# Where four query products of the next block stand: two in the attention steps and two behind output projection, or all four behind it

## The reference, cut to what matters

```
h = layernorm(x)                                # x: 4 x 2048 rows of 512
q = h @ Wq.T                                    # 1024 columns: 2 x 16 heads of 32
k, v = ctx @ Wk.T, ctx @ Wv.T                   # 154 context rows, 8 key/value heads
w = softmax(q1 k1) - lam * softmax(q2 k2)
a = (w v) * rsqrt(mean((w v)^2) + eps) * g * (1 - LAMBDA_INIT)
x = x + a @ Wo.T
h = layernorm(layernorm(x)) * g1 + b1ln         # second norm, then the norm inside the FFN
f = layernorm(gelu(h @ ternary(W1).T + b1))     # 2048 hidden columns
x = x + f @ ternary(W2).T + b2
```

## Time and profile before

| | |
|---|---|
| three runs | 2541.35, 2542.62, 2545.44 us (median 2542.62) |
| the profiled execution's span | 2537.8 us |
| PE, share of the span | 92% |
| DVE | 66% |
| ACT | 53% |
| POOL | 40% |
| HBM traffic | 36 GB/s over the span |

### The profile page before, as it was taken

One profiled execution on the slowest core, in us unless ns is written; L12 is line 12 of the kernel. 1 busy time (PEld: TensorE's weight loads), 2 busy tenths in 40 slices (PEclk: granted clock), 3 DMA queues, 4 the chain that ended last, 5 costly groups with the idle time before them and its releaser, 6 DMA issues.

```text
span 2537.8 us, 39240 instructions
## 1 busy us (share of the span) xinstructions
PE 2324.9 (92%) x13663; PEld 1092.8 (43%) x13663; DVE 1668.2 (66%) x2714; ACT 1340.0 (53%) x1943; POOL 1008.9 (40%) x823
## 2 busy tenths in 40 slices
PE   8489998999999898999989899998989999898988
PEld 5243544435353443535344353534435353444433
DVE  3866757485775748567574856757486675756563
ACT  3325465554656455465645546564554656465455
POOL 0221534435253443525344352534435253433416
PEclk9679999999999999999999999999999999999999
DMA  7222122120312212031221203122120312212000
GB/s 259 72 63 62 46 62 63 51 58 17 96 27 67 57 56 63 8 95 27 68 56 56 68 3 95 27 68 56 56 69 2 95 27 68 56 39 69 25 11 17
DMA packets 150890, 144.79 MB, mean 57 GB/s; under 512 B 66216, under 2 KB 117988, under 8 KB 150220
## 3 DMA queue, kind: packets, MB, share of 16 engines
q1 hardware_dynamic: 150732, 142.36, 19.6%
HBM read 70.56 MB, written 20.36 MB: 36 GB/s over the span
## 4 chain that ended last, share of the span: by engine, by line
PE 38%; issue 31%; DVE 14%; POOL 11%; ACT 4%; DMA 1%; POOLq 0%; SPq 0%; ACTq 0%; DVEq 0%
PE ps L1253 14%; PE ps L1263 13%; PE ps L1158 4%; DVE attn_raw L891 4%; POOL rstd L457 2%; POOL arena L481 2%; POOL q L462 2%; POOL arena L494 1%; POOL arena L490 1%; POOL rows L462 1%; DVE arena L853 1%; PE ps L1121 1%; ACT arena L642 1%; DVE attn_raw L886 1%; DVE p L873 1%
## 5 line engine op out<-in xcount | busy, mean ns | idle before, releaser
L494 POOL TENSOR_TENSOR arena<-arena 128x512 f32<-128x512 f32 x448 | 560.9, 1273 | 340.4 <-ACT arena L649 339.6
L1253 PE MATMUL ps<-rows,w1T 128*128 128x512 f16 x2048 | 484.5, 381 | 12.2 <-DVE rows L945 12.2
L853 DVE TENSOR_REDUCE arena<-ps 128x3 f32<-128x462 f32 (+1 forms) x704 | 405.4, 618 | 124.7 <-PE ps L1158 123.0
L1263 PE MATMUL ps<-w2T,arena 128*128 128x512 f16 x2048 | 478.8, 379 | 0.0
L642 ACT ACTIVATE arena<-ps,vec_cols,wstep 128x512 f32<-128x512 f32 x256 | 199.7, 780 | 447.4 <-PE ps L1253 404.2
L950 DVE SCALAR_TENSOR_TENSOR arena<-arena,vec_cols 128x512 f16<-128x512 f32 x256 | 196.9, 769 | 234.2 <-ACT arena L647 232.8
L1253 PEld LDWEIGHTS ps<-rows,w1T 128*128 128x128 f16 x2048 | 192.2, 98 | 216.1 <-DVE rows L945 21.6
L595 ACT ACTIVATE arena<-ps 128x512 f32<-128x512 f32 x128 | 76.2, 595 | 395.3 <-PE ps L1123 392.4
L1263 PEld LDWEIGHTS ps<-w2T,arena 128*128 128x128 f16 x2048 | 195.1, 98 | 207.1
L1158 PE MATMUL ps<-k_max,stack_raw 96*128 96x154 f16 x2048 | 208.4, 234 | 26.9 <-DVE arena L853 24.8
L462 POOL TENSOR_TENSOR q<-arena,q 128x512 f16<-128x512 f32 x64 | 74.2, 1160 | 396.5 <-ACT q L597 396.5
(11 more groups left out here) (163 smaller groups left out, 3387.1 us busy)
## 6 DMA issues: line engine op xcount, KB each, us to landing
arena<-in_x SPq DMA_DIRECT2D x32, 1024.0 KB, 6.1
stack_raw<-rows SPq DMA_DIRECT2D x384, 64.0 KB, 2.0
stack_raw<-q SPq DMA_DIRECT2D x384, 64.0 KB, 2.0
out<-arena SPq DMA_DIRECT2D x64, 256.0 KB, 2.1
arena<-in_L_ffn_w SPq DMA_DIRECT2D x8, 1024.0 KB, 10.6
k_max<-k_store SPq DMA_DIRECT2D x16, 490.0 KB
k_att<-k_store SPq DMA_DIRECT2D x16, 490.0 KB
v_att<-v_store SPq DMA_DIRECT2D x16, 384.0 KB, 5.8
```

The source lines that it names most:

```text
L494: ins = pool.tensor_tensor(acc[:, e, :], acc[:, e, :], src[:, j % 2, :], ALU.add)
L853: dve.tensor_reduce(negmax[:, tt, u0:u1], ps[:, B_O + tb % 2, 0:(u1 - u0) * S].rearrange("p (u s) -> p u s", s=S), AX.X, ALU.max, negate=T ...
L1253: ins = pe.matmul(ps[:, B_H + j % 2, :], w1T[:, k, j * P:(j + 1) * P], rows16[:, e, k, :], start=(k == 0 and e == 0), stop=(k == KD - 1 an ...
L1263: ins = pe.matmul(ps[:, tt, :], gg16[:, j % 3, e, tt * P:(tt + 1) * P], w2T[:, j, :], start=(j == 0 and e == 0), stop=(j == JH - 1 and e = ...
```

## The change

Two of the eight query products leave the attention steps, and a third moves one step later there. `q3` stands behind `v4` instead of `v3`; `q4` and `q5` stand behind output projection, ahead of `q6` and `q7`. The four late products alternate between two banks: `q5` moves to `B_L`, where `q7` is. The waits follow the banks: `q6` waits for the copy of `q4`, `q7` for that of `q5`. In the prologue `q5` waits for the row maxima of the first share, since it now shares their bank, and the second share of row scores waits for the copy of `q5`. On SP, the stack of pair 2 goes behind the residual load; on POOL, the remainder that stands between `power(1)` and `power(2)` is that of `q4` instead of `q6`.

```
 STEPS = [(w[0], int(w[1])) for w in (
-    "q0 q1 s0 q2 s1 v0 s2 v1 s3 v2 s4 a0 v3 q3 l0 s5 v4 q4 l1 s6 a1 v5 q5 s7 v6 a2 v7 a3").split()]
+    "q0 q1 s0 q2 s1 v0 s2 v1 s3 v2 s4 a0 v3 l0 s5 v4 q3 l1 s6 a1 v5 s7 v6 a2 v7 a3").split()]
...
-QLATE = 6
+QLATE = 4
...
-            return B_L if n in (1, QM - 1) else B_Q
+            return B_L if n in (1, QM - 3, QM - 1) else B_Q
...
                 if n == 1:
                     wait(pe, s_tmax, c, NT, 0)
-                elif n < QM - 1:
-                    wait(pe, s_q32, c, QM, {0: -1, 2: 1}.get(n, n))
+                else:
+                    wait(pe, s_q32, c, QM, {0: -1, 2: 1, 5: 0, 6: 5, 7: 6}.get(n, n))
...
                     for n in range(QLATE, QM):
-                        if n == QM - 1:
+                        if n == QLATE + 1:
                             wait(pe, s_ol2, i, KD, KD)
                         queries(i + 1, n)
...
+                    if n == QM - 3:
+                        pe.wait_ge(s_tmax, MSHARE[0][-1] + 1)
                     if n == QM - 1:
                         pe.wait_ge(s_tmax, MSHARE[1][-1] + 1)
                     queries(0, n)
...
                 elif what == "m":
+                    if n == 1:
+                        pe.wait_ge(s_q32, QM - 2)
                     if n == 2:
                         pe.wait_ge(s_q32, QM)
```

## The result

The changed kernel takes 2701.74 us (median of 4 runs, 2699.3 to 2711.75) against 2541.99 us for the kernel before beside it. The ratio is 1.0638, with a 95% interval of 1.0617 to 1.0659. The profiled execution's span is 2696.5 us, 158.7 above that of before. The forecast was 2684 us.

A forecast was written before the change was run, and what follows sets the result against it. No single engine was taken to bound the kernel; VectorE's order sets the attention steps' end. Per block 8.7 - 0.4 + 1.0 = 9.3 us, times 15 plus 2 in the prologue, gave about 2684 us, range 2640 to 2710.

The forecast's parts named there:

- The bound of the attention steps: Attention steps: VectorE's order of work sets their end, and PE runs along with a little slack.
- The control from the last block: Last block, no query product beside it: v5 to v7 normalisations take 8.65 us, against 9.01 with q5.
- The gain of 0.4 us: Attention steps, per block: DVE gains by less contention once POOL's remainder of q5 goes; bounds 0 and 5.2 us.
- The stack of pair 2: Ahead of h_hi: twelve DMAs issued one after another by SP land late, +8.7 us a block, lower end +7.7.
- the Trainium skill's dispatch figure: Some 50 ns dispatch per DMA: twelve would land some 3 us after the first, making the stack term 3.0 us.
- The PE side: Behind output projection: four products instead of two make h_hi 3.0 us later by PE alone, contained in the stack's wait.
- The clock: FFN's start: PE's 6.2 us idle leaves the 1.2 GHz level, costing 1.0 us a block, between 0 and 1.85.
- The prologue: Before the blocks, once: two exposed latencies of about 1 us each around q5, 2 us, between 0 and 4.
- The rivals: Four others: early stack landing 2584 us, 4%; PE-bound attention 2612, 6%; TensorE sets both places 2512, 2%; no effect, 1%.

The follow-up runs named there:

- e1_own_place: The changed kernel with pair 2 of the next block held in the space the FFN fills last, not in rows16: 2608.12 us, ratio 1.0269.
- e2_keep_clock: The changed kernel with 22 matmuls on constant weights ahead of the x_transposes in 14 blocks, to keep PE busy: 2683.54 us.
- e8_short_products: The kernel before the change, with q3, q4 and q5 of every block but the first over one of four contraction slices: 2532.22 us, ratio 0.9969.

## Why the prediction was right

**The bound of the attention steps** was read rightly. The control from the last block, 8.65 us without a product against 9.0 with one, was met to the hundredth in nine of the loop's 13 blocks: 8.65 or 8.66 from `v5` to `v7`. In all 13 PE is idle ahead of `v6` and the clock falls, which it did not before the change. In ten it is low for some 3 us, and the wait ahead of `v7` takes the loss up, as in the block at 1143 us, where L1203 took nearly double:

```profile
1191.36 1.94 PE L1203 MATMUL ps<-arena,v_att 128*32 128x512 f32 x8 [4.04 <-DVE attn_raw L886]
```

In the other three it is low for some 7 us, and the stretch takes 9.8 us. This is the loss that the prediction bounded by 0.2 a block and set to nothing; it is 1.2 in these three. Two rows of the stretches view, one of each kind:

```profile
1190.80:1194.00 3.20, 2.64 (x16) 0.60 (x16) 3.16 (x5) 0.00 (x0) 0.00 (x0) 0.50 0.42 102
```

```profile
873.30:880.00 6.70, 5.69 (x21) 1.19 (x21) 6.63 (x7) 0.00 (x0) 0.00 (x0) 0.50 0.48 99
```

The reading holds where DVE has the first norm. Iteration 14 has none, and there the stretch from `v3` to `v5` did fall, from 13.83 to 12.23 us.

**The gain of 0.4 us** in those steps is the term that failed in sign. The step said that what DVE gains is a POOL instruction less beside it, and counted only the instruction that the removal frees (L890). It left out that ACT reaches its squares earlier and that POOL's sum of squares then moves up beside L839. Measured in the loop's blocks: -0.35 us at L890, +0.95 at L839 and +0.27 on average by the clock. With iteration 14, and with 0.14 in the first stretch, the average over the 14 blocks is +0.8.

**The stack of pair 2** was mis-sized by 1.1 us. Its steps held one by one: POOL's slot (0.16 us from its end to the first issue), the pace, the 2.0 us of landing. I took the 8.59 us that pair 2 had needed before and read them as a later start of the twelfth DMA. It starts 7.0 us behind the first there too; what was long is that one issue, 1.55 us, and its landing, 3.1 us:

```profile
L399 SPq DMA_DIRECT2D stack_raw<-rows x12: 590/597/1552, 1123.4 to 1130.4; - x12
...
DMA to landing us min/median/max: 2.0/2.0/3.1
```

A packet of instructions ran beside it, and none did in the changed kernel, where the twelve took 7.65. The lower end, 7.7, was right, and 7.62 was measured. The sentence on the Trainium skill's dispatch figure cites a section on DMAs that GpSimd issues; it does not speak of SP's queue, and its 3.0 us did not come about.

**The PE side**, 3.0 us, hidden under the landing, came out as 2.86 in `e1_own_place`.

**The clock** was set to 1.0 us between 0 and 1.85. The FFN's opening lost 1.8, of which `e2_keep_clock` puts 1.6 on the clock: it stayed low for 4.1 us of the FFN, not 2.5, which cost PE 2.0 us, and only 0.4 of them were hidden.

**The prologue** was 2.2 us against 2. Per block the sum was 9.3 and is 10.3: one term too large by 1.1, two too small by 1.2 and 0.8. The profiled span is 17 us above the forecast one of 2679.3: 14 blocks times 1.0, iteration 0 with 2.3, and the last block with 1.0 that the forecast did not have. The mechanism of the large term was right; that the total came so near is in part luck, since its error and those of the two small terms have opposite signs. The rivals are out: `e1_own_place` shows the stack's landing to bind, and the attention steps gave nothing back.

Still open: what decides at which jumps, and ahead of which `v7`, the clock stays low for some 7 us, some 3 or not at all. That the instruction packets delay the stack's DMAs is read from where they stand in the traces, and no run tests it.

## What to carry to other kernels

Before moving a product to fill an engine's idle time, follow its result to the last reader of its buffer: here two products filled PE's 2.7 us of pauses and tied the FFN's input to twelve DMAs that one queue issues at 0.64 us each. Work taken off one engine also lets instructions of other engines start earlier; ask what they then run beside. If an engine's gap at the top of a loop says "issue", write the loop out on that engine alone and look: here it was worth 47 us, more than any order of the products tried.

## What the runs showed of the hardware that was not expected

- The jump back in PE's loop cost 1.84 to 2.35 us of idle time, and with the half clock behind it about 3.9 us a block; 12 of them made 47 us of 2542. The Trainium skill, page "Runtime: NRT & Kernel Launch", section "Instruction fetch mechanics", says that a taken branch whose target lies outside the current window of two pages forces a DMA fetch before execution can go on. The trace agrees for the body of 1747 instructions, with 9 instruction packets for each turn. It does not agree on the two pages, of 256 instructions each by that section: in `e8_short_products`, whose body in the trace is 54 instructions shorter, 1693, the packets and the gap were gone.
- The stack's DMAs were slow beside instruction packets. Behind 215 us in the kernel before, 34 of 714 issues of L399 took over 0.8 us, and 32 of the 34 overlapped a packet; of the 680 others 43 did. This is where they stand in the trace; no run separates the two.
- Four DVE instructions on 128x512 (L839) took 2.74 us beside one POOL tensor_tensor, 3.69 beside two and 4.54 beside three.
- ACT's queue and SP's issued the same DMAs side by side, at 0.64 and 0.68 us each, against 0.64 for SP's alone.
